# A selective-scan and expert kernel on one core: four of sixteen states get B times u from TensorE with B on a diagonal, and GpSimd takes two products with C of every quad

## What is computed

```python
x_dbl = einsum('bld,kd->blk', xn, x_proj_w)            # 128 ranks, 16 of B, 16 of C
delta = softplus(einsum('blr,dr->bld', x_dbl[..., :128], dt_proj_w) + dt_proj_b)
dae = exp(delta * A)           # A: 512 x 16, one decay for each of 16 states
dbx = delta * B * xn           # u = delta * xn; B differs by token and state
state = dae * state + dbx      # along 512 tokens, for each channel and state
y = sum over states of state * C, + xn * D_param
g = silu(mean of the two experts (of 8) that the gate picks: relu(xn @ W_e + b_e))
out = x + y * g
```

## Time and profile before

| | |
|---|---|
| median of 3 runs | 2283.3 us (2279.07 to 2288.0) |
| the profiled execution's own time | 2277.99 us |
| its span, first to last instruction | 2276.2 us |
| busy shares: PE, DVE, ACT, POOL | 81%, 87%, 61%, 83% |
| mean share of TensorE's clock granted | 0.93 |
| DMA | 641.47 MB, 282 GB/s on average |
| chain of work that ended last, by engine | DVE 28%, PE 24%, issue 23%, POOL 12%, ACT 9% |

### The profile page before, as it was taken

The page is one execution under the profiler, slowest core; times in us unless marked ns, Lnnn a source line. Parts: engine busy times, 40 slices in busy tenths (PEclk is TensorE's granted clock), DMA queues, the critical chain, the costliest instruction groups (busy, mean ns, idle before and its releaser), DMA issues.

```text
span 2276.2 us, 35000 instructions
## 1 busy us (share of the span) xinstructions
PE 1843.6 (81%) x8688; PEld 1192.7 (52%) x8688; DVE 1983.9 (87%) x3002; ACT 1378.6 (61%) x2370; POOL 1888.0 (83%) x1146
## 2 busy tenths in 40 slices
PE   2597988979788797888969888797987979888883
PEld 2364655546455564555546555465654646565552
DVE  3688898999889998899988989899888999989985
ACT  2465666666476665666656576565665666566663
POOL 2679889888888988889888988789888898898993
PEclk8698999989899998998989999899998999999997
DMA  5868798788968878798887978789797897987974
GB/s 212 291 229 336 238 345 279 266 323 256 365 199 308 310 259 327 232 327 290 262 309 240 367 245 295 278 258 367 222 323 258 267 352 228 360 269 265 337 253 127
DMA packets 281729, 641.47 MB, mean 282 GB/s; under 512 B 22529, under 2 KB 23041, under 8 KB 273297
## 3 DMA queue, kind: packets, MB, share of 16 engines
q1 hardware_dynamic: 187792, 445.84, 55.2%
q10 hardware_dynamic: 69120, 125.86, 15.6%
q0 software_dynamic: 24576, 67.13, 10.6%
HBM read 516.58 MB, written 122.16 MB: 281 GB/s over the span
## 4 chain that ended last, share of the span: by engine, by line
DVE 28%; PE 24%; issue 23%; POOL 12%; ACT 9%; ACTq 2%; DVEq 1%; DMA 1%; POOLq 0%; SPq 0%
PE z_ps L1028 12%; DVE scan_ps L881 7%; POOL dbx L444 6%; DVE p_sb L891 6%; DVE h_sb L881 4%; POOL xs_rows L470 4%; ACT scan_ps L597 3%; PE y_ps L1045 3%; PE proj_ps L980 2%; PE y_ps L1062 1%; POOL pp_sb L458 1%; DVE proj_ps L786 1%; PE proj_ps L972 1%; DVE stats L747 1%; PE xt_ps L1015 1%
## 5 line engine op out<-in xcount | busy, mean ns | idle before, releaser
L444 POOL TENSOR_TENSOR dbx<-b_sb,u_sb 128x1024 f32<-128x1024 f32 x512 | 1226.0, 2467 | 109.0 <-issue 41.1
L597 ACT ACTIVATE scan_ps<-delta,a_sb 128x512 f32<-128x512 f32 x1024 | 697.3, 688 | 645.2 <-DVE p_sb L891 612.2
L1028 PE MATMUL z_ps<-w_sb,xsT 128*128 128x512 f32 x1920 | 912.5, 620 | 111.1 <-ACT r_sb L618 111.0
L881 DVE TENSOR_TENSOR_SCAN scan_ps<-scan_ps,dbx 128x512 f32<-128x512 f32 x704 | 842.4, 1217 | 164.3 <-ACT scan_ps L597 138.6
L1028 PEld LDWEIGHTS z_ps<-w_sb,xsT 128*128 128x128 f32 x1920 | 360.8, 198 | 501.9 <-issue 501.5
L1045 PE MATMUL y_ps<-ident,p_sb 128*128 128x128 f32 x2816 | 430.3, 286 | 190.2 <-DVE p_sb L891 189.2
L458 POOL TENSOR_TENSOR pp_sb<-h_sb,c_sb 128x512 f32<-128x512 f32 (+1 forms) x256 | 404.9, 1582 | 163.1 <-PE y_ps L1062 143.8
L1045 PEld LDWEIGHTS y_ps<-ident,p_sb 128*128 128x128 f32 x2816 | 341.6, 146 | 354.4 <-DVE p_sb L891 238.3
L891 DVE TENSOR_TENSOR p_sb<-scan_ps,c_sb 128x512 f32<-128x512 f32 x704 | 473.4, 673 | 0.0
L881 DVE TENSOR_TENSOR_SCAN h_sb<-scan_ps,dbx 128x512 f32<-128x512 f32 x320 | 387.3, 1210 | 3.3 <-ACT scan_ps L597 3.2
L1030 PE MATMUL z_ps<-eb_sb,expert_hot 128*128 128x512 f32 x240 | 190.9, 796 | 0.0
(11 more groups left out here) (99 smaller groups left out, 1405.2 us busy)
## 6 DMA issues: line engine op xcount, KB each, us to landing
w_sb<-in_ew SPq DMA_DIRECT2D x240, 1024.0 KB
b_sb<-bc_rows SPq DMA_DIRECT2D x64, 1024.0 KB, 10.9
xs<-xs_rows ACTq DMA_DIRECT2D x240, 256.0 KB
ys_rows<-r_sb ACTq DMA_DIRECT2D x240, 256.0 KB
c_sb<-bc_rows SPq DMA_DIRECT2D x64, 768.0 KB, 14.7
xn<-in_x SPq DMA_DIRECT2D x16, 1024.0 KB, 15.7
c_sb<-bc_rows SPq DMA_DIRECT2D x64, 256.0 KB, 15.9
xo<-in_x SPq DMA_DIRECT2D x64, 256.0 KB
```

The source lines that it names most:

```text
L444: nc.gpsimd.tensor_tensor(dbx[:, k % DBX_PAIRS], b_sb[:, 2 * m:2 * m + 2, :], u_sb[:, dt % 2, :].unsqueeze(1).to_broadcast([P, 2, T]), ALU ...
L597: nc.scalar.activation(scan_ps[:, j % DA_BANKS, :], delta[:, dt % 2, :], ACT.Exp, scale=a_sb[:, dt, n:n + 1]).then_inc(da_ready, 1)
L881: nc.vector.tensor_tensor_scan(state, bank, dbx[:, j // 2 % DBX_PAIRS, r % 2, :], 0.0, ALU.mult, ALU.add).then_inc(scanned, 1)
L1028: nc.tensor.matmul(z_ps[:], xsT[:, slot, c, :], w_sb[:, i % WRING, c, :], start=(c == 0), stop=False)
```

## The change

- The dbx of states 2, 3, 10 and 11 (`PE_PAIRS`: pairs 1 and 5 of the eight in a `dt`) comes from TensorE. ScalarE lays B of each of these states on diagonals (`lay_diag`, 4 by 4 blocks a batch), TensorE turns u (`turn_u`, steps `U1` to `U3` and `NU0`), ScalarE copies it to `uT` (`keep_ut`), and TensorE multiplies, four matmuls a unit (`dbx_unit`, L1091 of the new file), into the unit's bank of `scan_ps`. The Exp of such a unit goes to a new tile `da_sb`; the scan reads decay from there and dbx from the bank. This is 16 units a batch, the last two of quads 0 and 2 of each `dt`. `dbx_unit(j + 2)` and `dbx_unit(j + 3)` stand on TensorE ahead of and behind `add_y(j)`, `j` being the quad's first unit.
- GpSimd makes 24 pairs of dbx a batch, in a ring of three, and two products with C in every quad, 32 a batch. VectorE makes the other 32.
- Expert tiles start at 6 and come every fourth unit, in two parts: two chunks at `j`, the rest at `j` + 1. `add_y` stands ahead of the steps and tiles of its `j`.
- `gate` makes `hot` with eight `tensor_scalar` in place of two `tensor_tensor`. Steps, gate, rank and the scatter of rows move by a few units; loads of B shrink to 12 rows, and SP's order is rewritten to match (not shown).

```diff
-DBX_PAIRS = 4
+DBX_PAIRS = 3
...
-STEPS = {2: "Z1", 9: "Z2", 16: "NT0", 18: "NT1", 20: "NT2", 22: "NT3", 24: "NX0", 26: "NX1", 28: "Z3",
-         35: "NK", 40: "NR", 41: "NS", 46: "NZ0"}
+STEPS = {2: "Z1", 10: "U1", 12: "Z2", 19: "NT0", 21: "NT1", 23: "NT2", 25: "U2", 27: "NT3", 29: "NX0", 31: "NX1",
+         33: "Z3", 39: "NK", 42: "U3", 45: "NR", 46: "NS", 48: "NZ0", 57: "NU0"}
...
-GATE_AT = 32
-RANK_AT = 38
+GATE_AT = 37
+RANK_AT = 42
 XD_AT = 11
 XD_ADD_AT = 1
 
-POOL_C = (1, 2, 1, 1, 1, 1, 1, 2, 2, 2, 1, 1, 1, 1, 1, 1)
+PE_PAIRS = (1, 5)
+
+DIAG_AT = (55, 56, 62, 63)
 
 TILES = 15
-TILE_AT = {8 + (i * 36) // 10: i for i in range(TILES)}
+TILE_AT = {6 + 4 * i: i for i in range(TILES)}
...
-SCATTER_AT = {10: (0, 1), 11: (2, 3, 4), 12: (5, 6, 7)}
+SCATTER_AT = {11: (0, 1), 12: (2, 3, 4), 13: (5, 6, 7)}
...
+    PE_STATES = [2 * m + i for m in PE_PAIRS for i in range(2)]
+    POOL_PAIRS = [g for g in range(UNITS // 2) if g % NPAIR not in PE_PAIRS]
+    KD = len(PE_STATES)
+    EB_ROWS = 64
...
         def on_dve(j):
-            return j % QUAD < ND[j // QUAD]
+            return j % QUAD < 2
...
-            def dbx_pair(b, k):
-                dt, m = k // NPAIR, k % NPAIR
-                if m == 0:
+            def dbx_pair(b, g):
+                dt, m = g // NPAIR, g % NPAIR
+                k = POOL_PAIRS.index(g)
+                if m == B_PAIRS[0]:
                     pool.wait_ge(u_ready, b * DT + dt + 1)
-                if dt == 0 and m % 2 == 0:
+                if dt == 0:
                     pool.wait_ge(b_in[m // 2], (b + 1) * 16)
-                pool.wait_ge(scanned, from_start((pair_no(b, k) - DBX_PAIRS + 1) * 2))
-                nc.gpsimd.tensor_tensor(dbx[:, k % DBX_PAIRS], b_sb[:, 2 * m:2 * m + 2, :],
+                if k >= DBX_PAIRS:
+                    pool.wait_ge(scanned, b * UNITS + 2 * POOL_PAIRS[k - DBX_PAIRS] + 2)
+                elif not is_first(b):
+                    pool.wait_ge(scanned, (b - 1) * UNITS + 2 * POOL_PAIRS[k - DBX_PAIRS] + 2)
+                nc.gpsimd.tensor_tensor(dbx[:, k % DBX_PAIRS], b_sb[:, B_PAIRS.index(m)],
                                         u_sb[:, dt % 2, :].unsqueeze(1).to_broadcast([P, 2, T]),
                                         ALU.mult).then_inc(dbx_ready, 1)
...
+            def lay_diag(b, i):
+
+                act.wait_ge(proj_used, next_step(b, "NX1") + 1)
+                act.wait_ge(pe_dbx, from_start((b - 1) * DT * KD + (DT - 1) * KD + i + 1))
+                n = R + PE_STATES[i]
+                for tt in range(TT):
+                    last = nc.scalar.activation(diag[:, i, tt, :], ident[:], ACT.Copy, scale=tok[:, tt, n:n + 1])
+                last.then_inc(diag_ready, 1)
+
+            def keep_ut(b, dt, no):
+                act.wait_ge(proj_done, no + 1)
+                act.wait_ge(pe_dbx, (b * DT + dt) * KD)
+                nc.scalar.activation(uT[:], proj_ps[:].rearrange("p (t q) -> p t q", q=P), ACT.Copy).then_inc(proj_used, 1)
+
             def da_unit(b, j):
                 dt, n = j // N, j % N
                 u = b * UNITS + j
                 if n == 0:
                     act.wait_ge(proj_used, delta_step(b, dt) + 1)
-                r = back(j, DA_BANKS)
-                before, of = (j - r, b) if j >= r else (j - r + UNITS, b - 1)
-                if on_dve(before):
-                    act.wait_ge(p_ready, from_start(dve_no(of, before) + 1))
+                if on_pe(j):
+
+                    k = pe_no(0, j) - 2
+                    if k >= 0:
+                        act.wait_ge(scanned, b * UNITS + pe_unit(k) + 1)
+                    elif not is_first(b):
+                        act.wait_ge(scanned, (b - 1) * UNITS + pe_unit(k + DT * KD) + 1)
+                    dst = da_sb[:, j % 2, :]
                 else:
-                    act.wait_ge(scanned, from_start(u - r + 1))
-                nc.scalar.activation(scan_ps[:, j % DA_BANKS, :], delta[:, dt % 2, :], ACT.Exp,
+                    r = back(j, DA_BANKS)
+                    before, of = (j - r, b) if j >= r else (j - r + UNITS, b - 1)
+                    if on_dve(before):
+                        act.wait_ge(p_ready, from_start(dve_no(of, before) + 1))
+                    else:
+                        act.wait_ge(scanned, from_start(u - r + 1))
+                    dst = scan_ps[:, j % DA_BANKS, :]
+                nc.scalar.activation(dst, delta[:, dt % 2, :], ACT.Exp,
                                      scale=a_sb[:, dt, n:n + 1]).then_inc(da_ready, 1)
...
+                        elif name == "NU0":
+                            keep_ut(b + 1, 0, no)
+                        elif name[0] == "U":
+                            keep_ut(b, int(name[1]), no)
...
+                    if j in DIAG_AT and nxt:
+                        lay_diag(b + 1, DIAG_AT.index(j))
...
-                nc.vector.tensor_tensor(hot[:, :, 0:TT], iota[:, 0:E].unsqueeze(2).to_broadcast([P, E, TT]),
-                                        topf[:, :, 0].unsqueeze(1).to_broadcast([P, E, TT]),
-                                        ALU.is_equal)
-                nc.vector.tensor_tensor(hot[:, :, TT:BLK], iota[:, 0:E].unsqueeze(2).to_broadcast([P, E, TT]),
-                                        topf[:, :, 1].unsqueeze(1).to_broadcast([P, E, TT]),
-                                        ALU.is_equal).then_inc(hot_ready, 1)
+
+                for k in range(2):
+                    for tt in range(TT):
+                        last = nc.vector.tensor_scalar(hot[:, :, k * TT + tt], iota[:, 0:E + 1], topf[:, tt, k:k + 1], None,
+                                                       ALU.is_equal)
+                last.then_inc(hot_ready, 1)
...
                 u = b * UNITS + j
                 q, r = j // QUAD, j % QUAD
                 dve.wait_ge(da_ready, u + 1)
-                if r % 2 == 0:
-                    dve.wait_ge(dbx_ready, pair_no(b, j // 2) + 1)
                 bank = scan_ps[:, j % DA_BANKS, :]
-                state = bank
+                state, decay = bank, bank
+                if on_pe(j):
+                    dve.wait_ge(pe_dbx, pe_no(b, j) + 1)
+                    decay, new = da_sb[:, j % 2, :], bank
+                else:
+                    if r % 2 == 0:
+                        dve.wait_ge(dbx_ready, pair_no(b, j // 2) + 1)
+                    new = dbx[:, POOL_PAIRS.index(j // 2) % DBX_PAIRS, r % 2, :]
                 if not on_dve(j):
                     dve.wait_ge(pp_ready, from_start(quad_no(b, q) - 1))
-                    state = h_sb[:, q % 2, r - ND[q], :]
-                nc.vector.tensor_tensor_scan(state, bank, dbx[:, j // 2 % DBX_PAIRS, r % 2, :], 0.0,
-                                             ALU.mult, ALU.add).then_inc(scanned, 1)
+                    state = h_sb[:, q % 2, r - 2, :]
+                nc.vector.tensor_tensor_scan(state, decay, new, 0.0, ALU.mult, ALU.add).then_inc(scanned, 1)
...
+            def turn_u(b, dt, no):
+                bank_free(no)
+                pe.wait_ge(u_ready, b * DT + dt + 1)
+                for tt in range(TT):
+                    last = nc.tensor.matmul(proj_ps[:, tt * P:(tt + 1) * P], u_sb[:, dt % 2, tt * P:(tt + 1) * P],
+                                            ident[:], start=True, stop=True, is_transpose=True)
+                last.then_inc(proj_done, 1)
+
+            def dbx_unit(b, j):
+                dt, i = j // N, PE_STATES.index(j % N)
+                if i == 0:
+                    pe.wait_ge(proj_used, (next_step(b, "NU0") if dt == 0 else step_no(b, f"U{dt}")) + 1)
+                if dt == 0:
+                    pe.wait_ge(diag_ready, b * KD + i + 1)
+                r = back(j, DA_BANKS)
+                before, of = (j - r, b) if j >= r else (j - r + UNITS, b - 1)
+                if on_dve(before):
+                    pe.wait_ge(p_ready, from_start(dve_no(of, before) + 1))
+                else:
+                    pe.wait_ge(scanned, from_start(b * UNITS + j - r + 1))
+                for tt in range(TT):
+                    last = nc.tensor.matmul(scan_ps[:, j % DA_BANKS, tt * P:(tt + 1) * P], uT[:, tt, :], diag[:, i, tt, :],
+                                            start=True, stop=True)
+                last.then_inc(pe_dbx, 1)
...
-            def tile(b, par, i):
+            def tile_first(b, par, i):
                 g = tile_no(b, i)
                 slot = (par * TILES + i) % 2
...
                 pe.wait_ge(r_ready, g)
-                for c in range(DT):
+                for c in (0, 1):
                     nc.tensor.matmul(z_ps[:], xsT[:, slot, c, :], w_sb[:, i % WRING, c, :],
-                                     start=(c == 0), stop=False)
-                nc.tensor.matmul(z_ps[:], expert_hot[:, par, i:i + 1].to_broadcast([P, P]), eb_sb[:],
-                                 start=False, stop=True).then_inc(z_done, 1)
+                                     start=(c == 0), stop=False, skip_group_check=True)
+
```

(21 more changed lines are left out.)

127 lines of the change are left out of this document (71 added, 56 removed).

## The result

The changed kernel takes 2783.8 us (median of 4 runs, 2781.49 to 2789.14), the kernel before 2281.2 in the same comparison: a ratio of 1.220, with an interval of 1.217 to 1.224. It is slower, as forecast, but by 22% where 4% was forecast. The forecast's range ended at 2455.

The account below looks back on a forecast made before the run. It took no engine to fill the batch, with 12 to 17 us lost in mutual waits. A ring of 113.8 us plus additions made 142.8 us a batch against 136.9, so about 2380 us, range 2210 to 2455.

Parts of the forecast that it names:

- The ring of TensorE quads: Between TensorE quads, eight times a batch: third unit's scan waits for TensorE's dbx, TensorE for VectorE's product; 14.2 us a round.
- the costly matmul: Rival: a unit's dbx matmuls on TensorE cost 1.24 us, not 0.88; 5.8 a batch more, 2472 us; chance 0.14.
- VectorE's insertions: Statistics 1.2, `delta_u` 1.45 and `rank` 2.9 between the third unit's scan and the second's product: +5.5 us a batch.
- `hot`, "1.2 less": At VectorE's gate: eight `tensor_scalar` take 1.1 us against 2.3 for the caught comparison, so 1.2 us less a batch.
- The ring's sum: TensorE's steps 12.16 us plus way out, scan, product and signals 2.07: 14.2 a round, 113.8 for eight rounds a batch.
- the low clock: Aside to a rival: low clock falling where TensorE sets the pace gives the same 2472 us; joint chance 0.14.
- A tile was taken at 3.66: TensorE's expert tile, start to start in the earlier timeline, 3.66 us; counted in the 12.16 of a round.
- Waits of the relu and of copies, "+4.0": A tile waits for the relu behind an Exp, 8 x 0.3, and steps wait for copies, some 1.6: +4.0 us a batch.
- Fewer bytes of B and later loads: Four of 16 rows no longer loaded, no idle time before GpSimd's products put down to a load: worth nothing.
- `copy_y`'s wait gone: Sign of being right: ScalarE's wait before `copy_y`, 104.9 us for TensorE in the kernel before, disappears.
- TensorE's waiting for more than some 20 us a batch in sum: Sign of being wrong: it would mean that another engine sets the pace.
- A `hot` comparison still at 2 us: Sign of being wrong, at VectorE's gate: a comparison of `hot` still takes 2 us.

Follow-up runs that it names:

- e3: Changed kernel with VectorE's product with C directly behind the scan, ahead of statistics, gate, rank, `delta_u` and combination: 2719.6 us.
- e2: Changed kernel with `hot` made by two `tensor_tensor` again, all else of the change kept: 2712.9 us.
- e8: Kernel before with only `hot` changed, from two `tensor_tensor` to eight `tensor_scalar`: 2356.4 us.
- e15: Changed kernel with whole tiles (second part directly behind the first) and `hot` by two `tensor_tensor`: 2695.0 us.
- e4: Changed kernel with the next batch's first rows loaded later, `ROWS_AT` from (57, 60) to (61, 63): 2725.9 us.
- e16: Kernel before with two products with C of every quad on GpSimd and `hot` in one instruction: 2403.0 us.
- e11: Kernel before with only GpSimd's share changed, two products with C of every quad on GpSimd: 2399.6 us.
- e6: Changed kernel with each of TensorE's four matmuls for B times u issued twice: 2884.8 us.

## Why the prediction was wrong

The direction held, and the mechanism in part. The ring of TensorE quads is there, the waits named are the ones that came (VectorE before L943's `h_sb`, released by L1091), and removing TensorE's products gives back more than any other single edit. But the ring's rung alone is 235 us, where the whole forecast was 99, and 192 us (155 + 37) came from parts that the forecast mostly put at nothing or gave no term. The pitch of the product's matmuls was sized right: eight rows take 0.90 us from start to start for a fourth unit (1219.11 to 1220.01) and 1.00 behind a tile, for 0.88 a unit forecast; the costly matmul of 1.24 is excluded. VectorE's insertions were 5.5 in the sum, and e3 with more moved gave 4.0. What failed:

- **`hot`, "1.2 less".** This step failed outright. It took 85.2 us, 5.3 a batch, for 40.8, 2.6, before: 2.8 more and not 1.2 less, worth 71 us in time (e2) and 79 in the kernel before (e8). The Trainium skill, "SBUF — State Buffer", section "SBUF: two separate sides", names as a party to the lock not only a VectorE operation with two SBUF inputs but also one in a two-port mode; the prediction weighed only the first. "VectorE: DVE Perf Modes" of the Trainium skill, section "Mode 2×_2P — use both read ports for one tensor", counts float32 `tensor_scalar` from and to SBUF among those that can use both ports, if the outermost dimensions of source and destination are even or equal. The trace agrees in that these operations are caught (two of the eight in the 5.49 us); whether by that mode no run here tells. The prediction also said that its sum was the same by both, "because TensorE sets the pace around the gate". That is wrong in a ring: VectorE's 5.49 came back as TensorE's idle 3.32.
- **The ring's sum took the full clock throughout.** Waits of TensorE had no price beyond their own length. After 3.32 and 3.47 us of idling a tile's first four rows took 3.75 and 3.38 instead of 1.88 us, at a granted clock of 0.50 and 0.52; rounds 4 to 8 have clocks of 0.86 to 0.93. TensorE is busy 141.5 us a batch, where 131 was forecast. The forecast had the low clock as a rival's aside, at 0.14 with the costly matmul, and gave it 92 us.
- **A tile was taken at 3.66.** It is 1.75 + 1.81 + 0.42 = 3.98 in the first round (1112.63 to 1114.38, 1115.26 to 1117.07 and 1117.07 to 1117.49), 0.3 more. In e15 the tile is whole and takes 1305.38 - 1301.43 = 3.95. So it isn't the parting. What both have, and the kernel before not, is the bias matmul over 64 rows. The weight loads show it, all 240 times: they idle 0.76 us before the load of 64 rows and 0.24 before that of 128, and in the first round the load starts only with its own matmul (1117.07). That it is the cause was not tried. 15 x 0.3 = 4.5 us a batch; two tiles a round bring the first round's 15.5 to 16.2. Waits of the weight loads, before and after:

```profile
PEld z_ps L1030 <- issue: 58.4, 240, 0.5
```

```profile
PEld z_ps L1122 <- issue: 182.0, 240, 0.8
```

- **Waits of the relu and of copies, "+4.0".** They had a term, but not their largest member: `ROWS_AT` stayed where it was while what it waits for moved by four units (e4, 58 us, 3.6 a batch). That was to be read in the code.
- **Fewer bytes of B and later loads were put at nothing, and the steps' places outside the ring had no term at all.** The ladder has +37 and +155 for them, in a kernel without TensorE's products. In the ring part of this would be hidden; how much isn't known, and what makes up the 155 stays open. The second figure overlaps with the tile's 0.3 and the rows' wait above.

The forecast of the signs was mixed. TensorE above 90% busy: it was 81%. `copy_y`'s wait gone: it moved, to 134.5 us released by the rows' turning. GpSimd idle 25 us or more: 168.7 - 112.4 = 56. "A `hot` comparison still at 2 us" was named as a sign of error, and it was one. So was TensorE's waiting for more than some 20 us a batch in sum: it waits 320.7 / 16 = 20 for `p_sb` alone, and idles (2782.2 - 2265.5) / 16 = 32 in all. VectorE's waits before the third scans, forecast at 2 to 3 us, are 3.8 to 7.2 from the first round's end on.

The range failed for one reason above the terms: each unknown was bounded by itself, at most 92 us, and the sum of several, all to the slow side, was not.

## What to carry to other kernels

When a product moves to the engine that stands at the other end of a dependence, price first its place in that engine's queue, and issue it as early as its buffer allows: the same matmuls one quad earlier were worth 153 us. Read every table of places that the change does not touch against what it moves. And before an operation's cost is taken from one trace, look whether it was caught behind another engine: a 0.2 us operation cost between 0.2 and 8.2 us a batch here, changed its cost with edits that had nothing to do with it, and one wait that lets it pass gave 117 us.

## What the runs showed of the hardware

- A VectorE operation on SBUF can stand through several GpSimd products in a row: 8.24 us in e16, where the earlier trace rows shows a wait that ends between two products (2.35). The long ones stand only where GpSimd's rows overlap by 0.6 us (28 of 28, in e11 and e16); that this decides was not tested.
- Eight `tensor_scalar` of 9 elements with the scalar in SBUF were caught like `tensor_tensor`: 85.2 us in the changed kernel, and 114.5 us with 8 elements in e8.
- A short pause of GpSimd at the right place costs it 0.26 us and saves VectorE 6.9 (8.24 to 1.34).
- TensorE with more work had a higher granted clock (0.942 in e6, 0.921 in the changed kernel), and 160 us of added busy time cost 101; how much of the difference is the clock no run tells.
- TensorE's granted clock was 0.50 and 0.52 behind idle times of 3.32 and 3.47 us, and back at 1.00 from 1204.7 to 1210.0.
- Before the weight load of a bias matmul over 64 rows the weight loads idle 0.76 us, before one over 128 rows 0.24, in each of 240 tiles.
